# Silu on ScalarE in place of tanh plus a VectorE operation, in a fused Mamba and mixture-of-experts block

## What is computed

```python
x = x + _layernorm(_L0_attn_ref(_layernorm(x), ...))   # a Mamba block: 512 channels, 16 states, scan over time
x = x + _layernorm(_L0_ffn_ref(_layernorm(x), ...))

# _L0_ffn_ref: 16 experts of width 128, every expert is computed for every token
topk_idx, topk_weight = _route(x, gate_weight, e_bias)
combine = (one_hot(topk_idx, E) * topk_weight[..., None]).sum(axis=1)
g = einsum('th,eih->tei', x, gate_proj)
u = einsum('th,eih->tei', x, up_proj)
act = silu(g) * u
expert_out = einsum('tei,ehi->teh', act, down_proj)
y = einsum('teh,te->th', expert_out, combine)
```

## Time and profile before

| | |
|---|---|
| median of 3 runs | 2791.8 us (2788.87 to 2792.28) |
| the profiled execution: time and span | 2792.0 us |
| VectorE (DVE) busy | 2455.6 us, 88% |
| TensorE (PE) busy | 2414.2 us, 86% |
| ScalarE (ACT) busy | 1628.2 us, 58% |
| GpSimd (POOL) busy | 1474.8 us, 53% |

### The profile page before, as it was taken

The page is one execution under the profiler, slowest core; times in us unless marked ns, Lnnn a source line. Parts: engine busy times, 40 slices in busy tenths (PEclk is TensorE's granted clock), DMA queues, the critical chain, the costliest instruction groups (busy, mean ns, idle before and its releaser), DMA issues.

```text
span 2792.0 us, 27042 instructions
## 1 busy us (share of the span) xinstructions
PE 2414.2 (86%) x8416; PEld 1179.1 (42%) x8416; DVE 2455.6 (88%) x3265; ACT 1628.2 (58%) x3312; POOL 1474.8 (53%) x516
## 2 busy tenths in 40 slices
PE   4556799898989989899998989899898989988898
PEld 1112254443534444354444435354444445444454
DVE  1799998989899998989989898999989899899642
ACT  3566565666666566665666656665666665654331
POOL 0355564646556564655555465565646556565511
PEclk9677899999999999999999999999999999999999
DMA  1532332425244252524435252433525233352221
GB/s 36 226 107 90 129 139 96 160 94 177 77 144 140 98 170 81 188 74 143 133 105 172 79 184 83 136 130 105 179 79 175 95 124 128 100 177 70 64 76 59
DMA packets 164811, 336.65 MB, mean 121 GB/s; under 512 B 15771, under 2 KB 73404, under 8 KB 156220
## 3 DMA queue, kind: packets, MB, share of 16 engines
q1 hardware_dynamic: 164668, 334.93, 35.8%
HBM read 291.35 MB, written 43.52 MB: 120 GB/s over the span
## 4 chain that ended last, share of the span: by engine, by line
PE 42%; DVE 39%; issue 10%; ACT 9%; DMA 0%; SPq 0%; DVEq 0%; ACTq 0%
DVE hs L872 17%; DVE hs L858 9%; PE Gp L416 8%; PE Up L424 7%; PE MY L434 7%; PE FP L343 5%; PE FP L353 4%; PE FP L379 3%; PE Y L446 3%; DVE th L987 3%; DVE th L992 3%; PE FP L361 1%; ACT XC L571 1%; ACT XB L519 1%; ACT DX L636 1%
## 5 line engine op out<-in xcount | busy, mean ns | idle before, releaser
L761 POOL TENSOR_TENSOR hs<-hs,Cb 128x2048 f32<-128x2048 f32 x256 | 1159.1, 4528 | 203.7 <-DVE hs L858 203.7
L501 ACT ACTIVATE dA<-dtr,A 128x512 f32<-128x512 f32 x1024 | 699.7, 689 | 771.3 <-DVE hs L872 768.7
L751 POOL TENSOR_TENSOR th<-th,cmb 128x512 f32<-128x512 f32 x256 | 325.4, 1271 | 1096.8 <-DVE hs L858 980.7
L872 DVE TENSOR_TENSOR_SCAN hs<-dA,carry,hs 128x512 f32<-128x512 f32 x512 | 627.2, 1264 | 31.7 <-ACT dA L501 31.4
L416 PE MATMUL Gp<-x2T,Wgu 128*128 128x512 f32 x1024 | 530.4, 642 | 129.2 <-DVE th L987 129.0
L872 DVE TENSOR_TENSOR_SCAN hs<-dA,hs 128x512 f32<-128x512 f32 x512 | 596.2, 1203 | 50.6 <-ACT dA L501 50.1
L858 DVE TENSOR_TENSOR hs<-dxr,Bb 128x2048 f32<-128x2048 f32 x256 | 586.6, 2292 | 13.4 <-DMA dxr<-dx_d 12.3
L434 PE MATMUL MY<-Wdn,th 128*128 128x256 f32 x2048 | 486.3, 380 | 0.0
L424 PE MATMUL Up<-x2T,Wgu 128*128 128x512 f32 x1024 | 486.2, 597 | 0.0
L434 PEld LDWEIGHTS MY<-Wdn,th 128*128 128x128 f32 x2048 | 383.6, 190 | 136.5 <-issue 84.6
L416 PEld LDWEIGHTS Gp<-x2T,Wgu 128*128 128x128 f32 x1024 | 183.6, 198 | 473.4 <-issue 259.1
(11 more groups left out here) (131 smaller groups left out, 1827.1 us busy)
## 6 DMA issues: line engine op xcount, KB each, us to landing
dtr<-dt_d SPq DMA_DIRECT2D x64, 1024.0 KB, 5.5
dxr<-dx_d SPq DMA_DIRECT2D x128, 512.0 KB, 7.2
cmb<-cm_d SPq DMA_DIRECT2D x256, 256.0 KB, 3.6
Wdn<-in_w_dn SPq DMA_DIRECT2D x256, 128.0 KB, 3.5
dt_d<-XB SPq DMA_DIRECT2D x16, 1024.0 KB, 4.3
dx_d<-DX SPq DMA_DIRECT2D x16, 1024.0 KB, 5.8
Bb<-bc_d SPq DMA_DIRECT2D x64, 256.0 KB, 3.1
Cb<-bc_d SPq DMA_DIRECT2D x64, 256.0 KB, 4.0
```

The costliest lines, as they stand in the source:

```text
L501: act.activation(dA[h % 2][:, :], dtr[:, M % 2, beta, :], ACT.Exp, scale=A[:, k:k + 1]).then_inc(s_dA, 1)
L751: pool.tensor_tensor(th[:, q % NTH, :], th[:, q % NTH, :], cmb[:, q % 2, :], ALU.mult).then_inc(m_a, 1)
L761: pool.tensor_tensor(hs[:, G % NH, :, :], hs[:, G % NH, :, :], Cb[:, s, :].unsqueeze(1).broadcast_to([P, NBETA, CH]), ALU.mult).then_inc(s ...
L872: dve.tensor_tensor_scan(hv, dA[h % 2][:, :], hv, first, ALU.mult, ALU.add).then_inc(s_h, 1)
```

## The change

ScalarE applies Silu to Gp itself. VectorE's `expert_gate` is gone; TensorE's next `gate` and VectorE's `expert_up` wait for ScalarE's activation (m_th) instead of m_v. The routing weights lose their factor 0.5.

```diff
PE 2414.2 (86%) x8416; PEld 1179.1 (42%) x8416; DVE 2455.6 (88%) x3265; ACT 1628.2 (58%) x3312; POOL 1474.8 (53%) x516 TensorE, gate(q)
                 if q >= 1:
-                    pe.wait_ge(m_v, q)
+                    pe.wait_ge(m_th, q)
PE 2414.2 (86%) x8416; PEld 1179.1 (42%) x8416; DVE 2455.6 (88%) x3265; ACT 1628.2 (58%) x3312; POOL 1474.8 (53%) x516 ScalarE, tanh(q)
-                act.activation(th[:, q % NTH, :], Gp[:, :], ACT.Tanh, scale=0.5).then_inc(m_th, 1)
+                act.activation(th[:, q % NTH, :], Gp[:, :], ACT.Silu).then_inc(m_th, 1)
PE 2414.2 (86%) x8416; PEld 1179.1 (42%) x8416; DVE 2455.6 (88%) x3265; ACT 1628.2 (58%) x3312; POOL 1474.8 (53%) x516 VectorE
-                dve.scalar_tensor_tensor(out=per_b(comb[:, :]), in0=per_b(sel), scalar=0.5, in1=wide(wr), op0=ALU.mult, op1=ALU.mult).then_inc(p_dve.sem, 1)
-
-            def expert_gate(q):
-                dve.wait_ge(m_th, q + 1)
-                dve.scalar_tensor_tensor(out=th[:, q % NTH, :], in0=th[:, q % NTH, :], scalar=1.0, in1=Gp[:, :], op0=ALU.add, op1=ALU.mult).then_inc(m_v, 1)
+                dve.scalar_tensor_tensor(out=per_b(comb[:, :]), in0=per_b(sel), scalar=1.0, in1=wide(wr), op0=ALU.mult, op1=ALU.mult).then_inc(p_dve.sem, 1)
PE 2414.2 (86%) x8416; PEld 1179.1 (42%) x8416; DVE 2455.6 (88%) x3265; ACT 1628.2 (58%) x3312; POOL 1474.8 (53%) x516
                 dve.wait_ge(m_u, q + 1)
-                dve.wait_ge(m_v, q + 1)
+                dve.wait_ge(m_th, q + 1)
PE 2414.2 (86%) x8416; PEld 1179.1 (42%) x8416; DVE 2455.6 (88%) x3265; ACT 1628.2 (58%) x3312; POOL 1474.8 (53%) x516
                 q = expert_at(G - 1)
-                if q is not None:
-                    expert_gate(q)
                 if S:
                     scan(G, 0)
```

More of the change, by code:

```diff
@@ L170, in sandwich_kernel @@
         p_act = Steps(sem('p_act'), ['xn0', 'xn1', 'rev0', 'rev1', 'nm', 'sq', 'ro', 'sum2', 'nm2', 'sq2', 'x2', 'x2T0', 'x2T1', 'sig', 'cmT'])
-        m_g, m_u, m_d, m_th, m_v, m_w, m_a = (sem(k) for k in ('m_g', 'm_u', 'm_d', 'm_th', 'm_v', 'm_w', 'm_a'))
+        m_g, m_u, m_d, m_th, m_w, m_a = (sem(k) for k in ('m_g', 'm_u', 'm_d', 'm_th', 'm_w', 'm_a'))
         z_act = Steps(sem('z_act'), ['my', 'nm', 'sq', 'zn'])
```

## The result

| | before | after |
|---|---|---|
| median | 2792.0 us (2788.9 to 2794.8) | 2848.1 us (2847.9 to 2850.6) |
| ratio to before | | 1.0204, 95% interval 1.0189 to 1.0218 |
| span of the profiled execution | 2792.0 us | 2846.0 us |

The forecast was 2800 in a range of 2766 to 2836. The direction was the likelier one (slower: 0.54), the size was not: 56 us instead of 8.

What follows compares the result with a forecast made beforehand. VectorE, 88% busy, looked like the bound, but TensorE's run held groups 0 to 6 and waits decided the rest. +1.6 us a round over twelve rounds (+19) less 11.5 outside gave +8: 2800 us, range 2766 to 2836.

Steps and rivals of the forecast that it cites:

- The bound of the kernel: VectorE is 88% busy, but no engine has much to give; in groups 0 to 6 TensorE is busy 69.4 of 70.6 us.
- The price of a load: ScalarE's table loads: 1283 ns each, next Exp 1.30 after load start; loads from 95 to 489, 505 us more ScalarE.
- the balance of one group: A group gains 0.60 us if ScalarE's last-place work P is under other VectorE work D + 0.54; otherwise the third scan waits.
- Groups 7 and 8: +2.1 us a round: x2T copy 1.4 later, TensorE's turn follows, then a load behind xd delays the third scan.
- Groups 0 to 6: 0: TensorE's run starts 1.4 us later behind the xT copy; a load gone before `f_silu` gives 1.3 to 1.4 back.
- Groups 10 and 11: +0.9: Per round: cmT copy 1.4 us later delays TensorE's fill, 1.0 given back for small pauses, then a load of 1.3 follows.
- a rival with 0.22: Clock drops more often behind TensorE's longer idle times: 2 us more a round, at most some 2.8; 2824 us, chance 0.22.
- A gain of 0.60 in every group that VectorE bounds: With its gate operation gone, VectorE gains the full 0.60 us in a group unless ScalarE makes the third scan wait.
- Outside the rounds: Sum -11.5 us: stage 1 -2, stage 2 -0.5, stage 15 -6, the last 182 us -3.
- The rival that TensorE's run shortens: Groups 0 to 6: gate product waits for ScalarE alone, the 2.84 us fill wait goes; 2766 us, chance 0.28.

Runs made afterwards that it cites:

- e1: The changed kernel with tanh (scale 0.5) in place of Silu: no table loads added, VectorE's gate operation still gone; 2756.5 us, 0.9878 of the kernel before.
- e3: The changed kernel plus four zero-weight matmuls on TensorE in its waits of groups 0 and 10; 2833.0 us, 1.0148 of the kernel before.
- e8: The changed kernel with Silu only for the experts of groups 0, 7 and 10, tanh in the other 13 (89 added loads); 2800.7 us, 1.0041.
- e9: The changed kernel with tanh in groups 0, 7 and 10, Silu in the other 13 (308 added loads); 2783.5 us, 0.9972.
- e4: The changed kernel with three ScalarE copies (xT 0, x2T 0, cmT) moved ahead of the table load and Silu, same 489 loads; 2786.8 us, 0.9983.

## Why the prediction was wrong

- **The bound of the kernel** held. In groups 0 to 6 TensorE's run sets the time: e1 frees VectorE by one operation in each of them and the piece falls by 0.1 us out of 4.2.
- **The price of a load** (1.28, and 1.30 to the next Exp) held; so did **the balance of one group**. Group 14 was forecast ready at 6.66 and waits 1.0 us, here on VectorE:

```profile
1692.45 2.46 DVE L872 TENSOR_TENSOR_SCAN hs<-dA,carry,hs 128x512 f32<-128x512 f32 x2 [1.02 <-ACT dA L501]
```

- **Groups 7 and 8** (+2.1, measured +2.4) held, by the mechanism given, the late x2T copy and the load behind xd:

```profile
1614.46 1.12 PE L389 MATMUL FP<-Cst,DX 128*128 128x128 f32 x4 [3.55 <-ACT x2T L644]
```

  The pause did not grow to 5.0 but stayed at 3.55, since TensorE itself came 1.4 us later to the turn ahead of it, against the third scan of group 7 (0.24 ahead of it instead of 1.67): its run had lost time on the way (next point). The waits for ScalarE within the run fell out otherwise than named, 4.0 us ahead of the third scan of group 6 instead of 2, and 2.0 instead of near 4 in group 7; their sum held:

```profile
1596.64 2.46 DVE L872 TENSOR_TENSOR_SCAN hs<-dA,carry,hs 128x512 f32<-128x512 f32 x2 [4.01 <-ACT dA L501]
...
1608.83 2.46 DVE L872 TENSOR_TENSOR_SCAN hs<-dA,carry,hs 128x512 f32<-128x512 f32 x2 [2.01 <-ACT dA L501]
```

- **The step that failed** is the price of the longer pauses in the two pieces "Groups 0 to 6: 0" and "Groups 10 and 11: +0.9". I shifted TensorE's work by the 1.4 us that the copy is late and let it run at full clock behind the pause. The rows show 1.6 us more for the gate matmuls in group 1 (3.58 against 1.98) and 1.65 for the fill and the sums in group 10 (1.34 + 0.31). That is 3.2 us a round against 2.9 missing in the two pieces, and 12 x 2.9 = 35 of the 46 us that the profiled execution lies over the forecast. For group 10 e3 shows it by taking it away. For groups 0 to 6 e3 shows it in the six rounds without low clock there: they take 0.9 less than in the changed kernel, of 1.3 to 1.4 that had come on top. e8 shows it a second time: in stages 5, 9 and 13 it has a stretch of low clock in group 0 and groups 0 to 6 take 77.7, in the other nine it has none and they take 76.3. (These 76.3 are 1.2 over e1: the copy is late, and since group 6 keeps its tanh, the load ahead of `f_silu` stays and gives nothing back.) The last 0.5 stays in e3 without low clock and is as long as TensorE's wait for ScalarE's copy in group 1.
- **Why it was missed.** The prediction knew the mechanism and set it aside as a rival with 0.22, against which it put that pauses of 1.1 had no low clock behind them. That was the wrong comparison, as the pauses were to become 2.0 and 2.5. The trace of the kernel before has pauses of that length, in group 13, where VectorE's work hides them and they cost nothing. Stage 8, then stage 9:

```profile
1473.36 1.98 PE L416 MATMUL Gp<-x2T,Wgu 128*128 128x512 f32 x4 [2.30 <-DVE th L987]
...
1635.58 3.59 PE L416 MATMUL Gp<-x2T,Wgu 128*128 128x512 f32 x4 [2.43 <-DVE th L987]
```

  In the six even stages the pause is 2.30 and the four gate matmuls behind it take 1.98, in the six odd ones it is 2.43 and they take 3.57 to 3.65. Read beside the forecast pauses, this makes low clock about as likely as not, and with it the sum is 12 x 3 = 36 us more, 2836. It could not have made it certain: in e8 the same pause in group 10 is 2.40 to 2.49 long, as in the changed kernel, and in none of its twelve rounds is there low clock behind it:

```profile
1622.34 1.98 PE L343 MATMUL FP<-xT,Win 128*128 128x512 f32 x4 [2.49 <-ACT cmT L658]
```

  So the length of a pause alone does not tell; what else decides stays open here. The rival was also priced too low: 2 us a round, at most 2.8 for two stretches (12 x 2.8 + 8 = 42, 2834), where they took 3.2.
- **A gain of 0.60 in every group that VectorE bounds** was too large a term. e1 shows 0.07 on average in groups 14 and 15, because L858 then runs into GpSimd. With all loads in place the effect was smaller, as ScalarE makes VectorE wait in half of these groups: 9, 12 to 13 and 15 came out as forecast to 0.15.
- **Outside the rounds** I forecast -11.5 and the profiled executions show -7. Of this, 3.9 lie ahead of the first scan, where the runs of this case differ by 8 us among themselves (86.1 to 93.9), and are no effect of the change. Stage 2 grew by 4.1, where I had 1.1: it has the same two new stretches of low clock as the full rounds. Stage 15 up to its last group fell by 1.8, where I had 6 for the stage, and what is behind it fell by 5.0, where I had 3.
- The rival that TensorE's run shortens is refuted: from the turn at 1537.90 to the copy of its last fill it took 64.5 us, not less than 63.2.

```profile
1602.43 0.60 ACT L565 ACTIVATE SZ<-FP 128x512 f32<-128x512 f32 x1 [0.70 <-PE FP L343]
```

- The 21 us that e8 and e9 together lack of the changed kernel's 92 lie in groups 10 and 11: over e1 these take 0.0 more in e8, 1.1 in e9 and 2.8 in the changed kernel, which is 1.7 x 12 = 20 us. The late cmT copy delays TensorE in e8 as well, but there ScalarE has no load behind the down product, TensorE has no low clock behind the pause, and the delay is covered. e9 (19.2) has the load and no late copy, e3 (19.3) the load and the late copy at full clock: the load is worth 1.1 and the late copy nothing more, until the low clock (1.63 by e3) comes behind it.

## What to carry to other kernels

A table load on an engine with spare time costs what waits behind it in program order: 92 us here, of which e4 takes back 61 by moving three copies of 0.6 us that another engine waits for ahead of it. When a pause of TensorE grows, look in the trace for pauses of the new length and at what its clock did behind them, and price low clock as a case with a fair chance: here pauses of 2.4 to 2.5 us in group 10 had it behind them in all twelve rounds of the changed kernel and in none of e8. When work is taken off VectorE, check what GpSimd is doing at the moment to which VectorE's next SBUF operation moves up.

## What was not expected of the hardware

- VectorE's product of two SBUF operands (128x2048) gets longer when its start falls together with a GpSimd product, and by most of the overlap: 2.38 us with an overlap of 0.24 (the kernel before, 35 of its 256), 2.61 with 0.47 and 2.86 with 0.71 (e1), against 2.28 with none. GpSimd's own product kept its 4.52. The scans, which read dA from PSUM, don't show it: in the kernel before those without a carry take 1203 ns all within a GpSimd operation (477 of them) and 1206 beside none (27).
- Over the span this turned 173.5 us of VectorE time saved into 89 us less busy time. Of the 84 us between, 23 are L858 (2292 to 2383 ns over 256) and 22 other VectorE operations that got longer (`f_dx` 2.32 to 2.66, the convolution 0.75 to 0.80 and others). The other 39 are counting: the durations of all records added up fall by 128 us, but busy time counts the stretches in which two records overlap once, and there are 39 us fewer of these.
- A load of 1.28 us in the wrong place costs 0.50 us of the kernel's time (e8), in a harmless place 0.09 (e9).
